# Small latent keys of batches 1 to 3 made between the experts and the last attention, and one mixed tile per visit in layer 2

## What is computed

```python
# layer 2, attention: 32 query heads of 16, 8 key/value heads, context of 512 tokens per batch
attn = softmax(einsum('bkgsd,bktd->bkgst', qh, kh) / sqrt(16))
out  = einsum('bkgst,bktd->bkgsd', attn, vh)
# layer 2, feed-forward: 8 experts, the 2 best per token, summed with softmax weights
# layer 3, attention over a latent context (16 heads)
q_r = einsum('bshq,hqr->bhsr', rope(hidden_q @ Wq @ w_kc_q), W_qr)
k_r = einsum('bld,hdr->bhlr', kv_r, W_kr)      # kv_r = rope(context): the "small latent keys"
ctx = softmax(q_r @ k_r.T) @ kv_r              # then through w_kc_kv and Wo
```

## Time and profile before

| | |
|---|---|
| median of 3 runs | 3749.89 us (3747.46 to 3751.34) |
| the profiled execution, its own time | 3746.39 us |
| its span in the trace | 3744.6 us |
| mean granted clock of TensorE | 0.976 of full speed |
| busy: PE, DVE, ACT, POOL | 3525.3 (94%), 2176.8 (58%), 1403.8 (37%), 627.6 (17%) us |
| share of the chain that ended last | PE 88%, DVE 6%, POOL 2%, ACT 1%, DMA 1%, issue 1% |

### The profile page before, as it was taken

How to read it: one execution, slowest core, us unless ns; L and a number is a source line. 1 busy time by engine, 2 the same in 40 slices (tenths; PEclk the granted TensorE clock), 3 DMA queues, 4 the chain that set the end, 5 groups by cost and what they waited for, 6 DMA issues and landing times.

```text
span 3744.6 us, 38074 instructions
## 1 busy us (share of the span) xinstructions
PE 3525.3 (94%) x12973; PEld 1932.4 (52%) x12974; DVE 2176.8 (58%) x3832; ACT 1403.8 (37%) x2908; POOL 627.6 (17%) x589
## 2 busy tenths in 40 slices
PE   5999999996889999599979999999999999999999
PEld 2444444442444444256634444444444445888888
DVE  7657676135677777411137776666675665655554
ACT  7525252111456666322224343444444443111111
POOL 5100000000132322211110100000000002544543
PEclk7999999998889999799989999999999999999999
DMA  7321311310422332455551201010101002121120
GB/s 238 135 75 68 130 68 68 116 45 23 109 53 57 80 75 57 173 157 165 159 186 55 72 26 38 26 38 26 39 26 38 26 26 101 57 68 57 68 79 23
DMA packets 81559, 292.46 MB, mean 78 GB/s; under 512 B 17897, under 2 KB 18793, under 8 KB 66545
## 3 DMA queue, kind: packets, MB, share of 16 engines
q1 hardware_dynamic: 74016, 267.74, 21.9%
q0 software_dynamic: 7376, 22.57, 2.0%
HBM read 246.74 MB, written 38.81 MB: 76 GB/s over the span
## 4 chain that ended last, share of the span: by engine, by line
PE 88%; DVE 6%; POOL 2%; ACT 1%; DMA 1%; issue 1%; SPq 0%; DVEq 0%; ACTq 0%; POOLq 0%
PE BM L2402 6%; PE BM L2472 6%; PE BM L460 6%; PE BR L460 6%; PE BM L2843 4%; PE BS L2843 3%; PE BR L2843 3%; PE BT L1616 3%; PE BT L2464 3%; PE BT L476 3%; PE BR L2481 3%; PE BS L476 3%; PE BM L2423 3%; PE BR L2055 3%; DVE NEG L1771 3%; PE BM L2044 3%
## 5 line engine op out<-in xcount | busy, mean ns | idle before, releaser
L2540 ACT COPY AR<-BM 128x512 f32<-128x512 f32 x320 | 187.2, 585 | 275.1 <-PE BM L2472 100.1
L228 POOL TENSOR_TENSOR RSTD<-VAR,HALF 128x4 f32<-128x4 f32 x31 | 33.5, 1082 | 1414.0 <-DVE VAR L2666 895.4
L2472 PE MATMUL BM<-AR 128*128 128x512 f32 x512 | 246.5, 593 | 0.0
L2402 PE MATMUL BM<-XT,AR 128*128 128x512 f32 x512 | 237.4, 607 | 0.0
L460 PE MATMUL BM<-XT,AR 128*128 128x512 f32 x512 | 230.2, 594 | 0.9 <-ACT AR L625 0.9
L460 PE MATMUL BR<-XT,AR 128*128 128x512 f32 x512 | 230.2, 593 | 0.0
L1709 ACT ACTIVATE PT<-BS 128x512 f32<-128x512 f32 x340 | 192.9, 600 | 90.6 <-PE BS L1606 85.2
L2546 ACT ACTIVATE AR<-BS,AR 128x512 f32<-128x512 f32 x128 | 86.8, 683 | 333.4 <-DVE AR L2636 333.4
L632 ACT ACTIVATE AR<-AR 128x512 f32<-128x512 f32 x256 | 182.6, 714 | 76.3 <-DVE AR L760 72.2
L2464 PEld LDWEIGHTS BT<-ID,AR 128*128 128x128 f32 x1024 | 127.3, 140 | 137.6 <-issue 133.1
L1771 DVE TENSOR_REDUCE NEG<-BM 128x2 f32<-128x1024 f32 x129 | 157.6, 1222 | 65.6 <-PE BM L1590 63.4
(11 more groups left out here) (460 smaller groups left out, 7241.2 us busy)
## 6 DMA issues: line engine op xcount, KB each, us to landing
AR<-l_wq_dram SPq DMA_DIRECT2D x32, 1152.0 KB, 5.1
AR<-l_w_dram SPq DMA_DIRECT2D x36, 1024.0 KB, 4.8
AR<-l_w_dram SPq DMA_DIRECT2D x64, 512.0 KB, 3.2
AR<-l_w_dram SPq DMA_DIRECT2D x40, 768.0 KB, 4.8
AR<-w2h SPq DMA_DIRECT2D x16, 1024.0 KB, 4.8
QS<-qx SPq DMA_DIRECT2D x32, 512.0 KB, 9.2
AR<-l_w_dram SPq DMA_DIRECT2D x8, 1408.0 KB, 8.3
made<-AR SPq DMA_DIRECT2D x40, 256.0 KB, 4.9
```

The source lines that it names most:

```text
L2402: last = nc.tensor.matmul(bank, WS[:, p % 2, at:at + P], XT[:, b % 2, kt, :], start=kt == 0, stop=kt == KT - 1)
L2472: last = nc.tensor.matmul(BM[:, L3[job] % 2, :], KVN[:, p // 8 * ST + lt, :], PROBT3[:, lt, :], start=lt == 0, stop=lt == ST - 1)
L2540: nc.scalar.copy(to, BM[:, L3[job] % 2, :]).then_inc(m_free, 1)
```

## The change

The keys of the pairs 8 to 31 (batches 1 to 3) leave the loop over pairs. Their weights (`WKR`, 512 KB) are loaded during the experts; after the last expert tile PE makes the 24 products through the two banks of `BM`, ACT copies each into one of six staging areas of four (`KST`), and SP stores these as they are free (six stores of 1 MB to `krd` in device memory). Two of the areas lie on `QB` and `RQ`, four on `W3`: ACT and DVE wait for the first two stores before they write there, and SP loads `W3` only after all six. In the loop SP then loads the keys of pair p - 1 into `KRT` (256 KB) once the scores of pair p - 2 have been made, and `scores` waits for that load. The keys of batch 0 stay where they were. The stores begin after six of the eight combined rows that batch 0 needs; before, SP went on (with the weights of pair 1, and then `W3`) after all eight.

In layer 2 every visit now mixes one tile, the one of two visits back, after its second pair. Where a memory of zeros signals that it is filled, an existing semaphore takes the place of one of its own.

```diff
@@ l2_tensor
-                        if h == 1 and tt % 2 == 1 and ST * n + tt > 1:
-                            for t in range(2):
-                                mix(*divmod(ST * n + tt - 3 + t, ST))
+                        if h == 1 and ST * n + tt > 1:
+                            mix(*divmod(ST * n + tt - 2, ST))
@@ moe_sync, after down(0, 0)
+            sp.dma_start(WKR, l3_wq[:, :, WK_AT:WK_AT + 2 * LR].rearrange("k p n -> p k n")).then_inc(l3_in, 16)
@@ moe_tensor_tiles, after the loop over tiles
+            pe.wait_ge(em.free, m.now() + 2)
+            pe.wait_ge(l3_in, 16 * (LH // 4) + 48)
+            for p in range(LATE_KEYS, NP3):
+                pe.wait_ge(m_free, L3["k", p] + 1)
+                nc.tensor.matmul(BM[:, L3["k", p] % 2, :], WKR[:, p % 8, :], KVT[:, p // 8 * S:(p // 8 + 1) * S], start=True, stop=True)\
+                  .then_inc(m_full, 1)
@@ moe_scalar, after the loop over tiles
+            for p in range(LATE_KEYS, NP3):
+                q, j = divmod(p - LATE_KEYS, 4)
+                act.wait_ge(m_full, L3["k", p] + 1)
+                nc.scalar.copy(KST[q][:, j, :], BM[:, L3["k", p] % 2, :]).then_inc(m_free, 1)
@@ areas of layer 3
+        LATE_KEYS = LH // 2
+        krd = nc.dram_tensor("krd", [NP3 - LATE_KEYS, P, S], F32, kind="Internal").ap()
+        WKR = area(MOE_END + 2 * B * S)(LH // 2, 2 * LR)
+        KST = [area(at)(4, S) for at in (W3_END + 3 * S * 2 + 2 * WSN, W3_END + 3 * S * 2 + 2 * WSN + 4 * S, 4 * S, 8 * S, 12 * S, 0)]
@@ l3_table
+            for p in range(LATE_KEYS, NP3):
+                put("m", "k", p)
...
-                if more:
+                if more and p + 1 < LATE_KEYS:
                     put("m", "k", p + 1)
@@ l3_sync
-            sp.wait_ge(yg_used, FIRST)
+            def store_keys(q):
+                sp.wait_ge(m_free, L3["k", LATE_KEYS + 4 * q + 3] + 3)
+                sp.dma_start(krd[4 * q:4 * q + 4].rearrange("k p n -> p k n"), KST[q]).then_inc(k3_stored, 16)
+
+            def keys(p):
+                sp.wait_ge(s_full3, ST * p)
+                sp.dma_start(KRT, krd[p - LATE_KEYS]).then_inc(k3_in, 16)
+
+            sp.wait_ge(yg_used, FIRST - 2)
+            for q in range(2):
+                store_keys(q)
             weights(1)
+            sp.wait_ge(k3_stored, 32)
+            for q in range(2, len(KST)):
+                store_keys(q)
             sp.wait_ge(es.free, NT + 2)
+            sp.wait_ge(k3_stored, 16 * len(KST))
...
             for p in range(2, NP3):
                 sp.wait_ge(m_full, L3["r", p - 2] + 1)
                 weights(p)
+                if p > LATE_KEYS:
+                    keys(p - 1)
+            keys(NP3 - 1)
@@ l3_tensor: scores, first tile
+                    if p >= LATE_KEYS:
+                        pe.wait_ge(k3_in, 16 * (p - LATE_KEYS) + 16)
@@ l3_tensor, between context of head 0 and of head 1
-                if more:
+                if p + 1 < LATE_KEYS:
                     small_keys(p + 1)
@@ l3_scalar, before big; l3_vector, before rotate
+            act.wait_ge(k3_stored, 32)
+            v.wait_ge(k3_stored, 32)
@@ the block
-        zero_ready = sem("zero_ready")
-            sp.wait_ge(zero_ready, 1)
+            sp.wait_ge(consts, 1)
```

More of the change, by code:

```diff
@@ L2277, in flamingo @@
         W3 = a(LH, D)
+        W3_END = a.here()
         ROPE = a(6, S)
@@ L2295, in flamingo @@
         SUM3, RS3, NEG3 = [a(2, 2 * ST).rearrange("p u (h s) -> p u h s", h=2) for _ in range(3)]
+        LATE_KEYS = LH // 2
+        k3_in, k3_stored = sem("k3_in"), sem("k3_stored")
+        krd = nc.dram_tensor("krd", [NP3 - LATE_KEYS, P, S], F32, kind="Internal").ap()
+        WKR = area(MOE_END + 2 * B * S)(LH // 2, 2 * LR)
+        KST = [area(at)(4, S) for at in (W3_END + 3 * S * 2 + 2 * WSN, W3_END + 3 * S * 2 + 2 * WSN + 4 * S, 4 * S, 8 * S, 12 * S, 0)]
+        assert len(KST) * 4 == NP3 - LATE_KEYS and W3_END == 16 * S
         def l3_table():
@@ L3160, in _ @@
         def _(pool):
-            nc.gpsimd.memset(ZERO[:, :], 0.0).then_inc(zero_ready, 1)
+            nc.gpsimd.memset(ZERO[:, :], 0.0).then_inc(consts, 1)
             nc.gpsimd.memset(HALF[:, :], -0.5).then_inc(consts, 1)
-            pool.wait_ge(consts, 1)
+            pool.wait_ge(consts, 2)
             norm_pool(pool)
```

## The result

Median 3704.95 us (3702.55 to 3707.57) against 3750.11 of before beside it: ratio 0.9881 [0.9864, 0.9898], 45.2 us less. The forecast was 54 less (3696, range 3674 to 3728). The profiled execution took 3705.75 (span 3703.9).

A forecast was written before the change was run, and what follows sets the result against it. The prediction took PE (TensorE) as the bound, 88% of the span, with waits for DVE in layer 2. Terms -32 - 20.6 - 1.5 = -54.1 us made the median forecast 3696 us, range 3674 to 3728.

The forecast's parts named there:

- 32 groups at 1.0: Layer 2: mixing one tile per visit saves 1.0 us in each of 32 groups, -32 us; ends +13 and -40.
- I credit these no more and no less: Layer 2's longer groups: 0.70 us of slack per visit takes most of DVE's normalising and routing, so same gain credited.
- The block of one tile: Layer 2's mix: a block of two tiles, 1.85 us, halves to 0.93 for one tile.
- The 12.26: Plain group of layer 2: PE's products, blocks and turns make 12.26 of 13.94 us, so at least 1.68 are lost.
- The 0.99 by the Trainium skill: Layer 2's mix: column tiles overlap, so a one-tile block lasts 0.99 us instead of 0.93; term -24 instead of -32.
- 24 keys at 0.86 in the loop: Layer 3's loop: 24 key products of 0.86 us leave PE's order, -20.6 us; bounds -20.6 and 0.
- The block in the gap, 0.88 per product: PE's gap between experts and layer 3: 24 key products take 21 us, hidden with 3 us to spare; term 0.
- Stores, `W3`, `KRT`: Around layer 3's start: key stores, then `W3` by 1961 with 29 us of cover, and `KRT` loads delay nothing; 0.
- Clock, -1.5: Layer 3's first turns and queries: a shorter PE rest may keep the clock up, -1.5 us (0 to -2.5).
- DVE stays the bound: Rival: in layer 2 PE waits as long elsewhere, so layer 2 gives 0; 3728 us, chance 0.15.
- Layer 2 gives more: Rival: layer 2's longer groups lose more than plain ones, 20 us more gain; 3676 us, chance 0.15.
- The three others: Rivals: key block outlasts gap, 3712, chance 0.05; layer 3's loop gives nothing, 3716, 0.04; `W3` late, 3764, 0.03.

The follow-up runs named there:

- the six: Six executions with the key block, 2.8 to 3.2 us of rest and the same instructions; prologues 26.73, 28.36, 28.36, 29.06, 26.72 and 28.36 us.
- the rest was filled: The changed kernel with three throwaway products behind the 24 key products: 3703.06 us, ratio 0.9879; with spread routing too: 3696.7, ratio 0.9864.

## Why the prediction was right, and where a size was off

The median lies in the forecast's own span (3684 to 3708; by its -40 for layer 2 the fast end would be 3688), near the slow end. The mechanisms came as written; one term was mis-sized, the -32 of layer 2, which measured -24.8.

- *DVE is what TensorE waits for in layer 2, and blocks of one tile end that.* Right: plain groups fell from 13.94 to 12.97 and their waits are gone, as forecast.
- *32 groups at 1.0.* The step that failed is "I credit these no more and no less" for the longer groups. Plain groups gave 0.93 to 0.97. Groups with a batch's normalisation gave up to 1.7, since TensorE stood still in them for some 2 us before, against 0.6 in a plain group. The routing groups gave 0.1 in three, against 3.0: over two full batches and part of a third that is as much as the 7 us that are missing. The cause given was 0.70 us of slack per visit; a burst of DVE of some 2 us is not paid from that, as TensorE can run only two units ahead. Before, the same bursts stood in part beside a double block. Spreading them gave 1.9 per batch back and 4.7 in all. The first of the three groups gave only 0.4; TensorE had stood still there for 0.9 us before, 0.6 of it for DVE.
- *The block of one tile.* Mis-sized: 1.00, not 0.93. The estimate for a plain group, 1.68 - 0.42 = 1.26 at most, loses 4 x 0.07, and 0.98 is left: the 1.0 between the ends was met for another reason than the one written. The 12.26 under the 1.68 is also luck: it leaves out the changeovers that the two old blocks have already (0.42) and takes the turns at 0.60 each, where they cost 0.35 and 0.41; the two cancel. The 0.99 by the Trainium skill (TensorE: Matmul & The Clock Gate, Part 3: Packing small matmuls) was right, as the 1.00 of the trace shows; that its term of -24 meets the measured -24.8 is chance, since the plain groups did give nearly 1.0 and most of the missing 7 us are DVE's bursts.
- *24 keys at 0.86 in the loop.* Right: 24 pairs are 0.86 shorter, and the loops of eight executions with the edit (1165.7 to 1168.4, mean 1167.1) lie 20.5 under the mean of four without (1187.6), 20.6 to 20.7 with equal falls of the clock.
- *The block in the gap, 0.88 per product.* Right: 0.90 (21.71 for 24), 2.9 us to spare. *Stores, `W3`, `KRT`:* right, nothing waits for them; `W3` has 27 us of cover where 29 were forecast.
- *Clock, -1.5.* The profiled execution shows -2.4, but the mean over the six is 27.93, 1.2 under the 29.12 of the earlier trace rows and 0.7 under the 28.62 of the kernel with the mix edit alone. Whether the clock falls in so short a rest differs from one execution to the next; the middle value was taken without a row, and came out near by luck. The rule from the Trainium skill (TensorE: Matmul & The Clock Gate, Part 1) that activity holds the clock up would make it -2.5; the trace agrees where the rest was filled, and only there in each execution.
- *Rivals.* "DVE stays the bound" came true for two routing groups of a batch's eight. "Layer 2 gives more" held for the groups with normalisation, but not in the sum. The three others did not show.

## What to carry to other kernels

When a producer and a consumer with two buffers run at similar rates, cut the work that stops the producer into the smallest block that does not lose its overlap: one tile here, while half a tile cost as much as a whole. Before crediting such a gain to every round, look for rounds in which the other engine has a burst longer than the buffers cover; such bursts have to be spread as well, and that alone brought the kernel from some 3704 to some 3696 us by the medians (4.7 us of it seen in layer 2). Read the burst's own rows first: one operation in it may be held up by a third engine. Work moved out of a full engine's loop into its gap comes back one for one, if its loads land early.

## Not expected of the hardware

Matmuls of 32 columns in further positions cost next to nothing beside the first: two heads 0.98 us, four heads 1.00 in a block. A small operation of DVE (0.17 us) took 1.15 to 1.38 beside a memset of GpSimd, 24 times of 24. With the same instructions and 2.8 to 3.2 us of rest, the granted clock fell in four executions of six, which moves the prologue by 1.6 to 2.3 us. A granted clock that had fallen in a rest of 14.17 us came back sooner after the restart (at 1939.6, 2.8 us) than one that fell during a rest of 3.73 (at 1945.9, 5.9 us), in one execution each.
